# A two-layer adapter kernel: layer 2 in three passes, and the order of work at both ends of layer 1

## The reference, cut to what matters

```python
# layer 1: x (8, 512, 2048), weight (8 adapters, 2048, 2048), one adapter for each of the 8 rows b
x1 = x + einsum('bsi,boi->bso', x, weight[itok_B_3_7])
# layer 2: one dense W (2048, 2048), bias, and a low-rank pair (rank 16) chosen for each b
base = einsum('bti,oi->bto', x1, W) + bias
h    = einsum('bti,bir->btr', x1, lora_A[ids])
out  = x1 + base + einsum('btr,bro->bto', h, lora_B[ids]) * 2.0
```

## Time and profile before

| what | value |
|---|---|
| median of three executions | 2571.18 us |
| the profiled execution, whole | 2572.88 us |
| its span, first to last instruction | 2571.0 us |
| PE busy | 2552.8 us, 99% |
| DVE / ACT / POOL busy | 65% / 34% / 49% |
| matmuls | 11232 |
| DMA | 648 MB, mean 252 GB/s |

### The profile page before, as it was taken

One profiled execution on the slowest core, in us unless ns is written; L12 is line 12 of the kernel. 1 busy time (PEld: TensorE's weight loads), 2 busy tenths in 40 slices (PEclk: granted clock), 3 DMA queues, 4 the chain that ended last, 5 costly groups with the idle time before them and its releaser, 6 DMA issues.

```text
span 2571.0 us, 30989 instructions
## 1 busy us (share of the span) xinstructions
PE 2552.8 (99%) x11232; PEld 2109.8 (82%) x11232; DVE 1671.4 (65%) x1882; ACT 876.4 (34%) x1159; POOL 1254.7 (49%) x1471
## 2 busy tenths in 40 slices
PE   8999999999999999999999999999999999999999
PEld 7888888888888888888888878888888888888887
DVE  5445455454454453454533368999998789999995
ACT  4232232232232242332422333333343433333333
POOL 3434424444444334334323466556666655556655
PEclk9999999999999999999999999999999999999999
DMA  9898889998999788899968887457777855546764
GB/s 353 314 301 297 300 285 279 300 284 282 270 304 328 267 285 279 272 286 276 288 195 197 237 277 265 139 172 248 263 247 250 290 168 175 162 143 201 234 226 143
DMA packets 238651, 648.03 MB, mean 252 GB/s; under 512 B 30116, under 2 KB 46500, under 8 KB 238500
## 3 DMA queue, kind: packets, MB, share of 16 engines
q0 software_dynamic: 123440, 393.28, 48.0%
q1 hardware_dynamic: 114772, 252.24, 30.6%
q10 hardware_dynamic: 288, 0.52, 0.1%
HBM read 433.07 MB, written 212.86 MB: 251 GB/s over the span
## 4 chain that ended last, share of the span: by engine, by line
PE 95%; DVE 2%; issue 1%; DMA 1%; POOL 0%; ACT 0%; SPq 0%; DVEq 0%; ACTq 0%
PE bank L839 18%; PE bank L840 18%; PE bank L841 18%; PE bank L869 12%; PE bank L873 12%; PE bank L871 12%; PE bank L824 1%; PE bank L823 1%; PE bank L887 1%; DVE c L800 1%; DVE xc L737 1%; DMA c<-x1s 0%; DMA wl<-w1s 0%; POOL wl L418 0%; DVE xq L723 0%
## 5 line engine op out<-in xcount | busy, mean ns | idle before, releaser
L839 PE MATMUL bank<-x_hi,w_hi 128*128 128x512 f32 x2048 | 797.9, 390 | 8.9 <-DVE w_lo L653 8.9
L418 POOL TENSOR_TENSOR wl<-wl 128x512 fp32r<-128x512 f32 x392 | 600.6, 1550 | 414.7 <-ACT wl L582 413.0
L840 PE MATMUL bank<-x_lo,w_hi 128*128 128x512 f32 x2048 | 797.5, 389 | 0.0
L841 PE MATMUL bank<-x_hi,w_lo 128*128 128x512 f32 x2048 | 797.4, 389 | 0.0
L869 PE MATMUL bank<-xc,wl 128*128 128x512 f32 x1568 | 611.6, 390 | 6.1 <-POOL wl L418 5.5
L873 PE MATMUL bank<-xc,wl 128*128 128x512 f32 x1568 | 610.8, 390 | 0.0
L871 PE MATMUL bank<-xc,wl 128*128 128x512 f32 x1568 | 610.6, 389 | 0.0
L536 ACT ACTIVATE w_hi<-w_raw 128x1024 fp32r<-128x1024 f32 (+1 forms) x258 | 258.0, 1046 | 970.6 <-PE bank L841 968.9
L758 DVE TENSOR_TENSOR x_raw<-bank,x_raw 128x512 f32<-128x512 f32 x128 | 88.5, 691 | 694.8 <-PE bank L841 644.4
L839 PEld LDWEIGHTS bank<-x_hi,w_hi 128*128 128x128 f32 x2048 | 384.9, 188 | 89.3 <-DVE w_lo L653 9.3
L840 PEld LDWEIGHTS bank<-x_lo,w_hi 128*128 128x128 f32 x2048 | 385.0, 188 | 79.9
(11 more groups left out here) (45 smaller groups left out, 1667.1 us busy)
## 6 DMA issues: line engine op xcount, KB each, us to landing
w_raw<-w0T SPq DMA_DIRECT2D x254, 512.0 KB, 7.8
wl<-w1s SPq DMA_DIRECT2D x392, 256.0 KB, 2.8
xss<-x_raw POOLq DMA_DIRECT2D x256, 256.0 KB, 4.4
w1s<-q_raw POOLq DMA_DIRECT2D x196, 256.0 KB, 7.3
q_raw<-w1T POOLq DMA_DIRECT2D x96, 512.0 KB, 9.8
xq<-xss POOLq DMA_DIRECT2D x40, 1024.0 KB, 7.0
x1s<-x_raw POOLq DMA_DIRECT2D x128, 256.0 KB, 2.9
c<-x1s POOLq DMA_DIRECT2D x32, 1024.0 KB, 7.2
```

The costliest lines, as they stand in the source:

```text
L418: pool.tensor_tensor(w[:, 1], w[:, 1].bitcast(F32), w[:, 0].bitcast(F32), ALU.subtract).then_inc(wl_ready, 1)
L839: pe.matmul(sums[s][:], w_hi[s][:, k, :], x_hi[:, k, :], start=(k == 0), stop=False)
L840: pe.matmul(sums[s][:], w_hi[s][:, k, :], x_lo[:, k, :], start=False, stop=False)
L841: mm = pe.matmul(sums[s][:], w_lo[s][:, k, :], x_hi[:, k, :], start=False, stop=(k == KT - 1))
```

## The change

- **Start.** VectorE writes zeros into the last two k blocks of `x_lo`; PE multiplies them 14 times into a bank that layer 1 does not use, before its first real matmul. VectorE waits for these (`zeros_used`) before it writes the true low part there, at x piece 7.
- **Tiles 0 and 1** are multiplied together for the first half of k (x pieces 0 to 3: tile 0's k pair, tile 1's k pair), then tile 0's second half, then tile 1's. Tile 1's w now also comes in quarters, in the order of `W_FIRST`, and x pieces are issued later. `w_done(n - 2)` replaces `w_total(n - 1)`; for tile 2 it means that six quarters' low parts are made. `add_h(0)` comes after both tiles.
- **a_hi(0), a_lo(0)** move from before tile 0's work to after its x1 parts.
- **load_c(0, 3, 0)**, C's first load, moves ahead of the stores of tile 127.
- **add_terms(2, h)** moves from after step 0's four sums to before step 0.
- **Layer 2's tiles** go in three passes of four k. For m = 0: high by high, w low by x high, w high by x low; for other m: high by high, w high by x low, w low by x high. PE waits only for w's high part (`wl_hi_done`) before the first pass, for `wl_ready` before the pass that uses w's low part, for `xc_hi_done` in pass one and `xc_ready` in pass three.

```diff
+        W_FIRST = [(0, 0), (1, 0), (0, 1), (1, 1), (0, 2), (0, 3), (1, 2), (1, 3)]
         def w_count(n, part):
-            return (n + 1) * PARTS + part + 1 if n > 0 else part + 1
+            if n < 2:
+                return W_FIRST.index((n, part)) + 1
+            return len(W_FIRST) + (n - 2) * PARTS + part + 1
+        def w_done(n):
+            return w_count(n, w_parts(n) - 1)
@@ SP
+                    for i, (first_n, part) in enumerate(W_FIRST if n == 0 else ()):
+                        sp.dma_start(w_raw[first_n][:, ks], ...).then_inc(w_first[first_n][part], 16)
+                        for c in ((), (2,), (3,), (), (4, 5), (6, 7), (), ())[i]:
+                            load_x_first(c)
                     if n >= 2:
-                        sp.wait_ge(w_ready, w_total(n - 1))
+                        sp.wait_ge(w_ready, w_done(n - 2))
@@ POOL
                     pool.wait_ge(x1_sum, n + 1)
+                    if n == TILES - 1:
+                        load_c(0, 3, 0)
                     pool.dma_start(x1s[b, t], x1_raw[s][:]).then_inc(x1_stored[s], 16)
...
-            pool.wait_ge(tile_done, TILES)
-            load_c(0, 3, 0)
@@ ACT (DVE in the same order, with the low parts)
             for c in range(XC):
                 x_hi_part(0, c)
-                if c % 2 == 0:
-                    w_hi_part(0, c // 2)
-            for part in range(PARTS):
-                w_hi_part(1, part)
-            a_hi(0)
+                if c in (0, 2):
+                    w_hi_part(*W_FIRST[c])
+                    w_hi_part(*W_FIRST[c + 1])
+                if c in (4, 6):
+                    w_hi_part(*W_FIRST[2 + c // 2])
+            for i in (6, 7):
+                w_hi_part(*W_FIRST[i])
@@
-                    if t == 0 and b > 0:
-                        h_hi(b - 1)
+                    if t == 0:
+                        if b > 0:
+                            h_hi(b - 1)
                         a_hi(b)
@@ DVE
+            dve.memset(x_lo[:, KT - 2:].bitcast(F32), 0.0).then_inc(zeros_ready, 1)
             for c in range(XC):
+                if c == XC - 1:
+                    dve.wait_ge(zeros_used, 1)
                 x_lo_part(0, c)
@@
             h_lo(NB - 1)
+            for h in range(SPLITS):
+                add_terms(2, h)
@@
-                    if m == Q - 1:
+                    if m == Q - 1 and s > 0:
                         for h in range(SPLITS):
                             add_terms(s + 2, h)
@@ PE
+            pe.wait_ge(zeros_ready, 1)
+            for i in range(WARM):                       # WARM = 14
+                mm = pe.matmul(banks[7][:], x_lo[:, KT - 2, 0:P], x_lo[:, KT - 1, :], start=(i == 0),
+                               stop=(i == WARM - 1))
+            mm.then_inc(zeros_used, 1)
@@
                         for k in range(KT):
+                            add_first(n, k)
+                    if n == 1:
+                        for c in range(XC // 2):
+                            for i in range(2):
+                                for k in range(c * KX, (c + 1) * KX):
+                                    add_first(i, k)
+                        for i in range(2):
+                            for k in range(HALF, KT):
+                                add_first(i, k)
                     if n > 0:
                         add_h(n - 1)
@@
-                    pe.wait_ge(wl_ready, n + 1)
-                    for k in range(Q):
-                        if m == 0 and k % (Q // SPLITS) == 0:
-                            pe.wait_ge(xc_ready, s * SPLITS + k // (Q // SPLITS) + 1)
-                        pe.matmul(bank[m][:], w[:, 0, k, :], x[:, 0, k, :], ...)
-                        pe.matmul(bank[m][:], w[:, 0, k, :], x[:, 1, k, :], ...)
-                        mm = pe.matmul(bank[m][:], w[:, 1, k, :], x[:, 0, k, :], ...)
+                    pe.wait_ge(wl_hi_done, n + 1)
+                    for p, (w_part, x_part) in enumerate(((0, 0), (1, 0), (0, 1)) if m == 0 else
+                                                         ((0, 0), (0, 1), (1, 0))):
+                        if w_part == 1:
+                            pe.wait_ge(wl_ready, n + 1)
+                        for k in range(Q):
+                            if m == 0 and k % (Q // SPLITS) == 0 and p != 1:
+                                pe.wait_ge((xc_hi_done, xc_ready)[x_part], s * SPLITS + k // (Q // SPLITS) + 1)
+                            mm = pe.matmul(bank[m][:], w[:, w_part, k, :], x[:, x_part, k, :], ...)
```

More of the change, by code:

```diff
@@ L89, in build @@
     XS = XC + 1
+    WARM = 14
     def scratch(name, shape):
@@ L190, in build @@
         w_loaded = [[sem(f"w_loaded{s}_{part}") for part in range(PARTS)] for s in range(2)]
-        w_first = [sem(f"w_first{part}") for part in range(2 * PARTS)]
+        w_first = [[sem(f"w_first{n}_{part}") for part in range(2 * PARTS)] for n in range(2)]
+        zeros_ready = sem("zeros_ready")
+        zeros_used = sem("zeros_used")
         w_hi_done = sem("w_hi_done")
@@ L468, in _ @@
                     if n == TILES - 3:
[L469 removed]
+                        pool.wait_ge(w_ready, w_done(TILES - 1))
                         load_xq(0, 1)
@@ L530, in w_hi_part @@
                 s = n % 2
-                if n == 0:
-                    act.wait_ge(w_first[part], 16)
+                if n < 2:
+                    act.wait_ge(w_first[n][part], 16)
                 else:
-                    act.wait_ge(w_loaded[s][part], (n + 1) // 2 * 16)
+                    act.wait_ge(w_loaded[s][part], n // 2 * 16)
                 ks = w_ks(n, part)
@@ L738, in xc_lo @@
                                   ALU.subtract).then_inc(xc_ready, 1)
+            dve.memset(x_lo[:, KT - 2:].bitcast(F32), 0.0).then_inc(zeros_ready, 1)
             for c in range(XC):
+                if c == XC - 1:
+                    dve.wait_ge(zeros_used, 1)
                 x_lo_part(0, c)
[L742 to L746, removed]
+                if c in (0, 2):
+                    w_lo_part(*W_FIRST[c])
+                    w_lo_part(*W_FIRST[c + 1])
+                if c in (4, 6):
+                    w_lo_part(*W_FIRST[2 + c // 2])
+            for i in (6, 7):
+                w_lo_part(*W_FIRST[i])
             for b in range(NB):
@@ L766, in _ @@
                         x_lo_part(b + 1, XC - 1)
-                    if t == 0 and b > 0:
-                        h_lo(b - 1)
+                    if t == 0:
+                        if b > 0:
+                            h_lo(b - 1)
                         a_lo(b)
@@ L832, in _ @@
                         pe.wait_ge(x1_sum, n - 1)
[L833 to L839, removed]
-                        pe.matmul(sums[s][:], w_hi[s][:, k, :], x_lo[:, k, :], start=False, stop=False)
-                        mm = pe.matmul(sums[s][:], w_lo[s][:, k, :], x_hi[:, k, :], start=False,
-                                       stop=(k == KT - 1))
-                        if k == KT - 1:
-                            mm.then_inc(tile_done, 1)
-                        elif t == NT - 1 and k % KX == KX - 1:
-                            mm.then_inc(x_free, 1)
+                        for k in range(KT):
+                            add_first(n, k)
[7 more added lines that the diff above has]
+                                add_first(i, k)
                     if n > 0:
```

42 lines of the change are left out of this document (25 added, 17 removed).

## The result

The changed kernel took 2562.94 us in the median of 7 executions (2561.91 to 2564.53), the kernel before 2571.08 us in 7 beside it (2568.56 to 2573.80). The ratio is 0.9968 with a 95% interval of 0.9957 to 0.9980: faster, by 8.1 us in the medians and by 5 to 11 by the interval. Forecast were 10.4 us. The profiled execution took 2562.13 us, 10.75 less than that of before; its span, 2560.6 us, is 10.4 shorter. One execution of the kernel before (3203 us) and one of the changed kernel (4615 us) ran at a mean clock of 0.75 and 0.71 and are left out of all ratios and means.

The account below looks back on a forecast made before the run. PE's matmuls were taken as the bound, busy 99% of the 2571.0 us span, with some 27 us open to edits of waits. Gains of 1.0 + 4.4 + 5.0 = 10.4 us gave 2560.8 us, 8 in 10 between 2558.8 and 2565.5.

Parts of the forecast that it names:

- the likeliest case: Whole kernel: the summed gain of 10.4 us holds, with a time of 2559.8 to 2562.5 us; chance 0.60.
- Three passes, waits: Layer 2 after its beginning: PE's waits for low parts go, gaining 5.0 of 5.3 us.
- The check beside it: Layer 2, window 2000 to 2500: 14 matmuls under layer 1's 2208, or 3.2 us, against 3.0 from the places there.
- Three passes, the matmuls: Layer 2: the same twelve matmuls in another order cost and gain nothing, 0 us.
- Rival E: Layer 2: the new order of matmuls itself costs time, making the kernel slower, 2582 us at 2%; chance 0.05.
- Rival D: Layer 2: VectorE is the bound, so the 5.0 us becomes 0 to 2, 2564 to 2566 us; chance 0.09.
- add_terms(2) earlier: Where layer 2 begins: PE's 2.95 us wait and the 1.45 us of slow clock after it go, 4.4 us.
- Warm-up: Start: fourteen matmuls of zeros raise the clock before the first real matmul at 8.92, gaining 2.2 us.
- Sharing x: Start, tiles 0 and 1: every low part comes 0.6 us or more ahead of PE, gaining 0.2 us.
- What is given back at tile 2: Start: tile 2's w is asked for later, so add_h(0) starts 0.2 to 0.5 us late.
- What is given back at tile 3: Start: W blocks land 1.2 to 2.4 us later, so the start keeps 1.0 us, between 0.2 and 1.4.

Follow-up runs that it names:

- start_only: The changed kernel with its three edits on layer 2 undone, so only the start's changes remain: 2572.8 us, ratio 1.0004.
- sum_early: The kernel before with only add_terms(2, h) moved to before step 0: 2568.24 us, timed once.
- c_early: The kernel before with only C's first load moved ahead of tile 127's stores: 2566.83 us, timed once.
- both: The changed kernel with VectorE's first sum_q one tile later and PE's add_h(0) only after tile 2: 2561.82 us, ratio 0.9965.
- ids_early: The changed kernel with the second ids' load issued right behind the first two pieces of x instead of last: 2569.97 us.
- again: The changed kernel once more, nothing edited: 2563.94 us, ratio 0.9972 to the kernel before.
- no_warm: The changed kernel without the 14 products of zeros and their waits: 2563.01 us.
- warm7: The changed kernel with 7 products of zeros instead of 14: 2563.07 us.
- passes: The kernel before with only layer 2's three passes and their waits from the changed kernel: 2565.39 us, ratio 0.9977.
- a_back: The changed kernel with a_hi(0) and a_lo(0) put back before tile 2's work: 2562.58 us, one execution.

## Why the prediction was right, and which terms were off

The forecast was faster, at 2560.8 us; measured were 2562.94 and 2563.94. Both lie in the range for 8 in 10 (2558.8 to 2565.5) and above the likeliest case's own, 2559.8 to 2562.5: 8.1 and 7.4 us were gained instead of 10.4. By the steps of the prediction:

- **"Three passes, waits"** (5.0 of 5.3). The waits are gone as said, but for slips that sum to 0 to 1.1 us in the ten kernels with passes. Four profiled kernels without the passes (before, `start_only`, `sum_early`, `c_early`) took 1064.87, 1063.78, 1064.07 and 1063.13 us from the 160th matmul to the last, mean 1063.96; the ten with them take 1059.2 to 1060.5, mean 1059.8. That is 4.15 us. My 5.3 was the highest of four: the waits were summed in one execution, and their places and sizes differ from one to the next. (The check beside it is off too: by the same starts the places between 2000 and 2500 us make 2.8, not 3.0.)
- **"Three passes, the matmuls"** (0). Right: 2206 in 500 us in either kernel with passes, two under the 2208 of layer 1. Without the late ones, the matmuls of layer 2 start 0.2267 us apart in both orders. Rival E is refuted. (160 in 36.27 us give 0.2267 as well, not the 0.2265 of the prediction, which counted those at a window's edges; the matmuls then need 2546 us, not 2544.) Rival D too: VectorE is busy 458 of 500 us and the waits went all the same.
- **"add_terms(2) earlier"** (4.4). 4.7 against the profile of before, 2.45 against an execution whose clock did not fall. The mechanism was right, and the slow clock's 1.45 (1.8 by the starts: 4.7 less the 2.95 of the wait), booked as if every execution had it, is there in most, not in all. And "If the moved add_terms alone failed, the load would still give 2.3 of the 4.4" was too low: the load alone gives it all. I took it 11.26 us long in its new place too; it took 6.9, and `add_terms` then has 4.2 us to spare.
- **"Warm-up"** (2.2). Right in itself: all real matmuls are fast. The first came at 9.10 instead of 8.92.
- **"Sharing x"** (0.2). "Every low part comes 0.6 us or more ahead" was wrong. I took tile 1's first w to land like the rest; ScalarE had to wait for it until 9.61 (10.12 in `both`), and PE lost 0.4 to 1.2 us there.
- **"What is given back at tile 2"** (0.2 to 0.5). 0.30 in the first profile. Tile 2's w was requested at 21.56 and landed 4.0 to 4.7 us later, with the burst at 23.26 behind it:

```profile
DMA to landing us min/median/max: 4.0/4.3/4.7
```

 This is the 4.5 of the earlier trace rows that I chose. The Trainium skill, "DMA: Bandwidth & Descriptors", section "Queues, rings and completion order", has each engine go round robin between the queues with work. This row does not go against it. In `ids_early`, where the burst was first, 6.3 and 9.3 us are more than equal shares would give: a half is 0.5 MB, 1.3 us at the 413 GB/s of the windows above, so one equal partner adds some 1.3 to the first half's 4.0 and 2.5 to the second's, 5.3 and 6.5 (an estimate). The measurement decides; where the other 1 and 3 us come from was not settled.
- **"What is given back at tile 3"** (start keeps 1.0). This is the step that was off. I had the W blocks late by 1.2 to 2.4 us; `sum_q` began late by 1.9 (changed), 3.7 (again), 3.7 (`start_only`), 2.1 (`no_warm`), 3.2 (`warm7`). I had counted tile 2's w as what delays them, asked for 1.2 us later (it was 2.05, 21.56 against 19.51), and not the load of `ids` that stands last in SP's list, behind the loads that the change puts there. POOL began 1.4 to 2.3 us later in these five, on average 1.9 of the 2.9 by which `sum_q` was late; the rest is a longer way of the blocks themselves. How much the load of `ids` alone accounts for is not shown: without it POOL would wait for x piece 6, and `ids_early` won 1.3 us there. On average tile 3 begins at 45.62 in the three profiles with the changed start, at 45.30 in the four with the old one (44.96, 45.31, 45.59, 45.34): the start keeps nothing on average, -0.3 us instead of +1.0, with a scatter of 1 us either way. Three profiles against four do not rule out the 1.0, but the times of `start_only` show no gain either.

Made anew: the place where layer 2 begins costs 4.7 in 33 of 40 executions and 2.45 in 7, if every fall is there, 4.3 on average. -0.3 + 4.3 + 4.15 = 8.2 us, less some 0.5 for the falls in 5 of 14 executions of the changed kernel (1.4 us longer each), and with the 0.4 outside the span: 8.1. The medians say 8.1 and 7.4. That the profiled pair differs by my 10.4 is in part luck: its start kept 0.5 and its later layer 2 5.3 us, where the averages are -0.3 and 4.15. Where the clock falls in those 5 executions stays open: none of them was profiled. `passes`, with the old start, has none in 10, which points to the changed start, but 5 of 14 against 0 of 10 is thin. Nor was it settled why the W blocks land up to 1.8 us apart from one execution to the next.

## What to carry to other kernels

Where a matmul stream is full, look at what it needs at its turn and not at what a tile needs in all: an order that uses the part made first and the part made last at the end took away all but some 1 us of layer 2's waits behind its beginning, and no engine got faster. An advance at a kernel's start is kept only as far as the next load on the way lets it; follow every load that stands behind the ones you add to a queue, the tiny ones too, up to who starts on it. And size waits by several executions: with 1 or 2 us each they come and go, and with them the clock.

## What the runs showed of the hardware

- Standstills of PE of 1.3 (`c_early`), 1.5 (before), 1.6 and 2.1 (`again`), 2.5 and 2.8 us (`start_only`), start to start, were followed by matmuls at the fast spacing; such of 3.2 (before), 4.9 (`warm7`) and 6.0 us (`ids_early`) by a granted clock of 0.58, 0.51 and 0.50. In `warm7` the matmuls ahead of it had been slow already. The same wait stood on either side in two executions (2.5 and 3.2 us), and that made 2.25 us of difference.
- Products of zeros raised the clock as those of data do: the last five of fourteen are 0.23 apart in `start_only`; in the changed kernel all fourteen are 0.43 apart, and behind them its real matmuls run at the spacing of 0.23 us from the first, at 9.10; ten of the kernel before and of `no_warm` are 0.43 apart.
- Requested 1.2 to 1.7 us ahead of four loads of 0.5 MB on POOL's queue, half a tile of w took 4.0 to 4.7 us; requested 0.7 to 1.3 us behind them, 6.3 to 9.3. In `a_back`, requested only 0.3 us ahead, the second half took 6.4. Here some 2.5 us in the order of two requests went with 5 to 7 us of the kernel, in one execution.
- The load of C, issued ahead of a tile's stores, landed in 6.6 and 6.9 us; issued behind them, in 11.3 to 12.0.
- The same kernel's first tiles moved by 1.8 us between two executions, by when the W blocks landed.
